# Normalisation in two batches of images, deviations by a matrix product, last output chunk in halves by images

## The reference

```python
def _gn(v, G=32, eps=1e-05):           # per image, over groups of 4 channels and all pixels
    g = v.reshape(B_, G, C_ // G, H_, W_)
    m = jnp.mean(g, axis=(2, 3, 4), keepdims=True)
    s = jnp.var(g, axis=(2, 3, 4), keepdims=True)
    return ((g - m) / jnp.sqrt(s + eps)).reshape(v.shape)

def step(h, xr):                        # 32 steps over lines, per direction
    out = _gru_step(xi, h, wih, whh)    # r, z = sigmoid(x W + h W); n = tanh(x W + r * (h W))
    ctx = out ...                       # (1 - z) * n + z * h
    h_new = jnp.tanh(_conv1d(ctx, cw, cb))   # three taps along the line
    return (h_new, ctx)

x = x + (einsum(concat([ctx_above, ctx_below, ctx_left]), w_comb) + b_comb)
```

## Time and profile before

| | |
|---|---|
| median of 3 runs | 341.11 us (340.92 to 341.3) |
| profiled execution | 341.09 us |
| its span, first to last instruction | 339.3 us |
| TensorE busy | 321.5 us (95%), 2723 products |
| VectorE busy | 291.5 us (86%) |
| ScalarE busy | 253.9 us (75%) |
| GpSimd busy | 11.0 us (3%) |
| DMA | 10.61 MB; HBM read 6.16 MB, written 4.19 MB |

### The profile page before, as it was taken

The page is one execution under the profiler, slowest core; times in us unless marked ns, Lnnn a source line. Parts: engine busy times, 40 slices in busy tenths (PEclk is TensorE's granted clock), DMA queues, the critical chain, the costliest instruction groups (busy, mean ns, idle before and its releaser), DMA issues.

```text
span 339.3 us, 7733 instructions
## 1 busy us (share of the span) xinstructions
PE 321.5 (95%) x2723; PEld 261.0 (77%) x2723; DVE 291.5 (86%) x781; ACT 253.9 (75%) x593; POOL 11.0 (3%) x24
## 2 busy tenths in 40 slices
PE   0589999999999999999999999999999999999995
PEld 0237678888888888888888888888888888874443
DVE  1889999999999999999988888889898888894542
ACT  5979899999888887887777777777777777767600
POOL 2540000000000000000000000000000000000000
PEclk9999999999999999999999999999999999999999
DMA  7900000000000000000000000000000000000655
GB/s 297 411 19 4 0 2 0 2 3 1 2 2 0 3 2 1 2 0 3 0 0 0 0 0 0 0 0 0 0 0 0 0 0 0 0 2 0 198 149 149
DMA packets 11252, 10.61 MB, mean 31 GB/s; under 512 B 2529, under 2 KB 9825, under 8 KB 11233
## 3 DMA queue, kind: packets, MB, share of 16 engines
q1 hardware_dynamic: 11232, 10.36, 9.1%
HBM read 6.16 MB, written 4.19 MB: 31 GB/s over the span
## 4 chain that ended last, share of the span: by engine, by line
PE 87%; ACT 4%; DVE 3%; DMA 2%; issue 1%; POOL 1%; POOLq 0%; SPq 0%; ACTq 0%; DVEq 0%
PE rz_bank L909 23%; PE conv_bank L909 18%; PE rz_bank L912 11%; PE n_bank L909 11%; PE conv_bank L912 9%; PE n_bank L912 6%; DMA x<-x_dram 2%; PE rz_bank L1017 1%; PE rz_bank L1021 1%; PE rz_bank L1019 1%; PE n_bank L1017 1%; PE n_bank L1021 1%; PE n_bank L1019 1%; ACT w_parts L470 1%; PE conv_bank L1021 1%
## 5 line engine op out<-in xcount | busy, mean ns | idle before, releaser
L909 PE MATMUL conv_bank<-ctx_store,w_parts 128*128 (+1 forms) x558 | 106.7, 273 | 0.4
L909 PE MATMUL rz_bank<-x_rows,w_parts 128*128 (+1 forms) x378 | 77.7, 273 | 1.0 <-DVE x_rows L662 0.5
L909 PE MATMUL rz_bank<-h_parts,w_parts 128*128 128x256 f16 x372 | 76.2, 273 | 0.3 <-DVE h_parts L771 0.3
L524 ACT ACTIVATE nval<-npre 128x256 f32<-128x256 f32 x93 | 38.6, 415 | 48.0 <-DVE npre L766 48.0
L512 ACT ACTIVATE rz<-rz_bank,descale 128x512 f32<-128x512 f32 x93 | 63.9, 687 | 8.4 <-PE rz_bank L909 1.6
L912 PE MATMUL conv_bank<-ctx_store,w_parts 128*128 (+1 forms) x279 | 66.0, 273 | 0.0
L909 PEld LDWEIGHTS conv_bank<-ctx_store,w_parts 128*128 128x128 f16 x558 | 53.8, 97 | 14.6 <-DVE ctx_store L759 1.9
L748 DVE SCALAR_TENSOR_TENSOR npre<-n_bank,descale,rz 128x256 f32<-128x256 f32 x93 | 44.9, 483 | 15.5 <-ACT rz L512 14.2
L529 ACT ACTIVATE hval<-conv_bank,biases,descale 128x256 f32<-128x256 f32 x93 | 51.4, 553 | 0.3
L912 PE MATMUL rz_bank<-x_rows,w_parts 128*128 (+1 forms) x189 | 51.5, 273 | 0.0
L909 PE MATMUL n_bank<-x_rows,w_parts 128*128 128x256 f16 (+1 forms) x192 | 47.1, 273 | 0.0
(11 more groups left out here) (99 smaller groups left out, 417.3 us busy)
## 6 DMA issues: line engine op xcount, KB each, us to landing
x<-x_dram SPq DMA_DIRECT2D x8, 512.0 KB, 8.3
out_dram<-x_rows SPq DMA_DIRECT2D x7, 512.0 KB, 3.3
ctx_store<-weights_dram SPq DMA_DIRECT2D x3, 576.0 KB, 5.1
out_dram<-x_rows SPq DMA_DIRECT2D x2, 256.0 KB, 2.6
ctx_store<-weights_dram SPq DMA_DIRECT2D x1, 192.0 KB, 12.0
biases<-biases_dram SPq DMA_DIRECT2D x1, 2.0 KB, 11.7
```

The costliest lines, as they stand in the source:

```text
L524: nc.scalar.activation(nval[k][:], npre[k][:], ACT.Tanh).then_inc(n_done[k], 1)
L909: last = nc.tensor.matmul(out, w_block(HI, k, n), parts(hi_or_lo), start=start, stop=stop and hi_or_lo == LO, skip_group_check=True)
```

## The change

**Two batches.** Mean, variance, power and shift are made for images 0 to 5 and then for 6 and 7 (`BATCHES`), each with semaphores of its own count. A new matrix `group_dev` = `unit_diag` - `group_avg`, built by GpSimd, gives the deviation from the group mean by one product; ScalarE squares it (`squared_dev`) and the variance is summed in PSUM by two products, of the channel variances and of the squares.

```diff
-            nc.tensor.matmul(avg_bank[:, 0:B], group_avg[:], meanvar[:, :, 0],
-                             start=True, stop=True).then_inc(mean_avg, 1)
-            warm(CHAIN_WARM)
-            pe.wait_ge(spread_done, 1)
-            nc.tensor.matmul(var_bank[:, 0:B], group_avg[:], dev[:], ...
+            def batch_means(batch):
+                images = slice(*BATCHES[batch])
+                by_act = sum(b < images.stop for b in ACT_IMAGES)
+                pe.wait_ge(aggr_done, images.stop - by_act)
+                pe.wait_ge(act_stats, 2 * by_act)
+                nc.tensor.matmul(dev_bank[batch][:, images], group_dev[:], meanvar[:, images, 0], ...
+                nc.tensor.matmul(mean_bank[batch][:, images], group_avg[:], meanvar[:, images, 0], ...
+                nc.tensor.matmul(var_bank[batch][:, images], group_avg[:], meanvar[:, images, 1],
+                                 start=True, stop=False)
+            def batch_variance(batch):
+                pe.wait_ge(spread_done, batch + 1)
+                nc.tensor.matmul(var_bank[batch][:, images], group_avg[:], dev[:, images],
+                                 start=False, stop=True).then_inc(var_avg, 1)
+            batch_means(0)
+            batch_variance(0)
+            batch_means(1)
+            batch_variance(1)
             turn_sums(1)
-            warm(TURN_WARM)
+            warm(5)
             spread_peaks(1)
-            warm(CHAIN_WARM)
-            pe.wait_ge(x_factor, 1)
-            warm(LAST_WARM)          # 7
+            pe.wait_ge(x_factor, 2)
+            warm(LAST_WARM)          # 4
```

```diff
 # ScalarE
-            for unit in range(2, UNITS.index("in 2")):
-                weights_hi(unit)
-            for k in (2, COMB):
-                magnitude_sums(k)
+            weights_hi(2)
+            squared_dev(0)
+            weights_hi(3)
+            weights_hi(4)
+            weights_hi(5)
+            magnitude_sums(2)
+            squared_dev(1)
+            magnitude_sums(3)
...
 # VectorE
-            for b in (2, 3, 5, 6, 7):
-                image_stats(b)
-            spread()
+            image_stats(2)
+            image_stats(3)
+            image_stats(5)
+            image_stats(6)
+            group_mean(0)
+            variance(0)
+            image_stats(7)
             weights_lo(UNITS.index("conv 1"))
-            variance()
-            sets_peak(1)
             weights_lo(UNITS.index("rec 1"))
-            shift()
...
+            shift(0)
+            normalise(2, edges)
+            group_mean(1)
+            variance(1)
+            normalise(3, edges)
+            normalise(4, edges)
+            sets_peak(1)
+            shift(1)
+            normalise(7, edges)
+            normalise(0, strip)
+            normalise(1, strip)
+            weight_scales(1)
             x_lo(FIRST_ROWS[0])
-            weight_scales(1)
+            x_lo(FIRST_ROWS[1])
+            x_lo(FIRST_ROWS[2])
             x_lo(FIRST_ROWS[3])
```

**Turn to the output.** In block (31, 2) the first four hidden products of direction 2 are issued ahead of the output products:

```diff
+                begun = j == 2 and isinstance(t, int) and t == STEPS - 1
+                if begun:
+                    hidden_gates_hi(2, STEPS - 1)
                     unit_ready("comb")
```

**Last chunk.** Both rows of images 0 to 3 and then of images 4 to 7 (`LAST_PARTS`) are multiplied into a bank each, summed, and stored singly:

```diff
-            for row in range(CHUNK_ROWS):
+            for part, (b, end) in enumerate(LAST_PARTS):
...
+            for part, (b, end) in enumerate(LAST_PARTS):
+                sp.wait_ge(y_summed, CHUNKS + part)
+                sp.dma_start(out_d[b:end, :, last * CHUNK_ROWS:CHUNKS * CHUNK_ROWS, :]
+                             .rearrange("b c h w -> c b (h w)"),
+                             y_sb[:, whole, b:end, CHUNK_ROWS * W:STORE_ROWS * W]).then_inc(y_stored, 16)
```

More of the change, by code:

```diff
@@ L382, in _ @@
                     .then_inc(y_stored, 16)
[L383 to L389, removed]
+            sp.wait_ge(y_summed, last)
+            sp.dma_start(out_d[:, :, (last - 1) * CHUNK_ROWS:last * CHUNK_ROWS, :].rearrange("b c h w -> c b (h w)"),
+                         y_sb[:, whole, :, 0:CHUNK_ROWS * W]).then_inc(y_stored, 16)
+            for part, (b, end) in enumerate(LAST_PARTS):
[3 more added lines that the diff above has]
+                             y_sb[:, whole, b:end, CHUNK_ROWS * W:STORE_ROWS * W]).then_inc(y_stored, 16)
+            sp.wait_ge(y_stored, 16 * (whole + 1 + len(LAST_PARTS)))
         @block.gpsimd
@@ L963, in input_products, with hidden_gates_hi, hidden_products @@
                     last.then_inc(n_ready[k], 1)
-            def hidden_products(k, s):
+            def hidden_gates_hi(k, s):
+                pe.wait_ge(h_hi_done[k], s)
+                for gate in range(2):
+                    passes(rz_bank[k][:, gate * COLS:(gate + 1) * COLS], k, GATES + gate,
+                           lambda part: h_parts[k][:, part, :], HI)
+            def hidden_products(k, s, begun=False):
                 def parts(part):
                     return h_parts[k][:, part, :]
-                pe.wait_ge(h_hi_done[k], s)
-                for gate in range(2):
-                    passes(rz_bank[k][:, gate * COLS:(gate + 1) * COLS], k, GATES + gate, parts, HI)
+                if not begun:
+                    hidden_gates_hi(k, s)
                 pe.wait_ge(h_lo_done[k], s)
@@ L1003, in convolution, with chunk_part @@
                 last.then_inc(conv_ready[k], 1)
-            def chunk_part(c, k, first=0, end=CHUNK_ROWS):
-                rows = slice(c * CHUNK_ROWS + first, c * CHUNK_ROWS + end)
-                out = y_bank[(c + first) % RING][:, 0:(end - first) * W * B] \
-                    .rearrange("p (h w b) -> p h w b", h=end - first, b=B)
+            def chunk_part(c, k, bank=None, b=0, end=B):
+                rows = slice(c * CHUNK_ROWS, (c + 1) * CHUNK_ROWS)
+                out = y_bank[(c if bank is None else bank) % RING][:, 0:CHUNK_ROWS * W * (end - b)] \
+                    .rearrange("p (h w b) -> p h w b", h=CHUNK_ROWS, b=end - b)
                 def ctx_part(p):
@@ L1088, in _ @@
             c = CHUNKS - 1
-            for row in range(CHUNK_ROWS):
-                pe.wait_ge(y_summed, c + row - RING + 1)
+            for part, (b, end) in enumerate(LAST_PARTS):
+                pe.wait_ge(y_summed, c + part - RING + 1)
                 for k in range(DIRS):
-                    last = chunk_part(c, k, row, row + 1)
+                    last = chunk_part(c, k, c + part, b, end)
                 last.then_inc(y_ready, 1)
```

141 lines of the change are left out of this document (82 added, 59 removed).

## The result

The changed kernel takes 342.49 us (median of 22 runs, 341.64 to 342.97), the kernel before 341.01 (22 runs). The ratio is 1.0037 with a 95% interval of 1.0031 to 1.0044: slower by 1.5 us, where 340.9 was forecast. The profiled execution took 342.26, its span 340.5 (before 339.3: +1.2). The front alone lost more than that; the two ends brought most of what was forecast of them.

The account below looks back on a forecast made before the run. The prediction took a chain of waits over VectorE, GpSimd and ScalarE to bound the kernel up to 39.6 us, then TensorE products. 341.09 + 0.6 (front) - 0.33 (turn) - 0.5 (last store) gave 340.9 us, range 339.8 to 342.9.

Parts of the forecast that it names:

- step 3: Front, VectorE's chain from the fourth weights_lo on: first x_lo at 24.9 instead of 24.23, +0.67; front +0.6 us.
- TensorE falls back: Rival: TensorE drops to 1.2 GHz in the front, five products take 2.1 instead of 1.1; 342.9 us, chance 0.16.
- Step 1: Front, TensorE reaching the first batch: deviation product at about 18.1 behind twelve slow warm-ups, variance(0) at 19.24.
- warm-up over sooner: Rival: fast spacing comes within the twelve front warm-ups, four take 0.85 less; front -0.25, 340.0 us, chance 0.16.
- step 2: Front, work queued behind new waits: image 7's statistics 2.4 us later, ScalarE idle 16.3 to 18.5, first power at 20.25.
- The power: GpSimd's power in the front: 1.24 for six columns and 0.41 for two, by column shares of 1.65; no wait added.
- the limit of 0.9: Front, GpSimd's second power, two columns: starts at 22.5, asked for at 23.4, so it may take 0.9 before it costs.
- The rival with two of 1.65: Power does not shrink with its columns: the second ends at 24.35, first x_lo at 25.8, +1.6; 341.9 us, chance 0.07.
- The turn: Loop to output products: four hidden products run in TensorE's 0.43 wait, gain 0.33 us, bounds 0 and 0.44.
- The last chunk: End of kernel: half stored after the first sum, last store only 128 KB, -0.5 us, bounds -0.6 and -0.1.
- the outer bound of +1.0: Last chunk's products: operand runs of 8 bytes taken as free, at worst a doubled read costing +1.0 us.
- The rival with the tail hidden: Gap products issued late and the half store landing as slowly as the whole: 341.7 us, chance 0.05.

Follow-up runs that it names:

- experiment 12: Changed kernel with image 7's statistics ahead of the first batch's mean and the square behind weights_hi 3 to 5, no added warm-ups: 340.24 us, in two groups.
- experiment 1: Changed kernel with nine more warm-up products, seven after batch_variance(0) and two ahead of batch_variance(1): 340.59 us, ratio to the kernel before 0.9982.
- Experiment 11: Changed kernel with image 7's statistics early, the square late, three warm-ups inside, six at the end, and first x_lo ahead of weight_scales(1): 340.30 us.
- experiment 7: Changed kernel with nine more warm-ups ahead of batch_variance(1) and image_stats(7) ahead of group_mean(0) and variance(0): 340.81 us, ratio 0.9989.
- experiment 10: Changed kernel with image 7's statistics ahead of the first batch's mean, square behind weights_hi 3 to 5, three warm-ups inside, six at the end: 339.52 us.
- experiment 4: Kernel before with only the four hidden_gates_hi products of direction 2 put ahead of the first output products: 340.61 us, ratio 0.9988.
- experiment 5: Kernel before with only the last chunk in halves by images and two stores of 128 KB: 340.60 us, ratio 0.9985.
- experiment 9: Changed kernel with 9 front warm-ups instead of 12, eight after batch_variance(0), two ahead of batch_variance(1): 341.42 us, in two groups.
- experiments 8: Changed kernel with 6 front warm-ups instead of 12, three after batch_variance(0), one ahead of batch_variance(1): 341.38 us, ratio 1.0008.
- old front with both ends: Kernel before with hidden products ahead of the output products and the last chunk in halves, nothing of the new front: 340.34 us, ratio 0.9979.
- experiment 3: Kernel before with the changed kernel's thinner warm-ups: 12 in front, none in the two places of four, 5 ahead of spread_peaks(1), 4 at the end: 341.09 us.

## Why the prediction was wrong

It moved by +1.5 where no measurable change was forecast, inside the range given.

**The step that failed** is the one that took TensorE's level as held through the front (step 3, and "they were at the fast spacing from 18.65"). Its mechanism stood among the rivals, *TensorE falls back*, with 0.16: five products at 2.1 (measured 2.31), 342.9 in all (342.49), decided by a spacing over 0.3 (0.43). The argument against it, "no stretch of more than 1.7 without a product", was no argument: the wait was 1.69 and the level fell, and in experiment 12 it fell without such a wait. What the runs support is in the rival's first sentences: where the old front had warm-up products in every microsecond, the new one has nothing but small float32 pairs from 17.2 to 22.2. The granted clock was 0.50 from 19.5 to 26.2, and experiment 1, which puts nine products into that stretch, shows the price, 1.90 of the 2.15. The Trainium skill (TensorE: Matmul & The Clock Gate, "A second HAM failure mode: psum-queue depth-cycling") has a level that goes back and forth with short idle times between groups. The trace of experiment 12 agrees in so far as the level fell with no idle time over 0.31; whether these short ones were its cause no run shows.

**Front without the clock.** The terms of steps 1 to 3 were about right where the level held: in experiment 1 the first batch comes behind twelve slow warm-ups at 18.22 (forecast 18.1), image 7's statistics at 19.62 (19.3), `x_hi` at 24.69 (24.4) and `x_lo` at 25.23 (24.9), with warm-ups that started 0.17 later than before. Step 1 let the variance product follow the square at once; two more pairs stand ahead of it in TensorE's queue, and `variance(0)` came 1.32 behind the first pair and not 1.14. In these traces the new front then costs 0.97 against the old one, 0.75 from the first warm-up on, against +0.6 forecast. By medians it is only 340.59 - 340.34 = 0.25. The rest is probably executions in which the warm-up ends earlier, as in the profiled run of the changed kernel; no such run of experiment 1 was traced. That was the rival *warm-up over sooner*; in the traced execution of the changed kernel it came true together with the fall-back, which no case had combined.

**What was queued behind the waits** (step 2) was right in kind. The prediction counted these stalls inside its +0.6 and did not ask for another order; taking both waits behind the work, with other warm-ups, brought 340.59 to 339.52 by medians and 341.29 to 340.45 in the traced executions. Experiment 11, nearly the same kernel, has 340.30.

**The power** took 1.33 for six columns and 0.80 for two, where the shares gave 1.24 and 0.41; the limit of 0.9 held and no wait came of it in the changed kernel. In experiments 7 and 10 to 12 six columns took 1.64 or 1.65, and VectorE waited 0.78 for them. The rival with two of 1.65 is out. The Trainium skill (GPSIMD Engine Reference, "Performance versus the Vector engine") has a cost for each element and, beside it, a dispatch and a join of the cores for each instruction. The rows agree that it does not go by the elements alone: 0.80 for two columns is more than half of the 1.33 for six.

**The turn**: forecast -0.33; the trace gives -0.27 to -0.32, experiment 4 -0.44. **The last chunk**: forecast -0.5; -0.46 in the trace and -0.45 in experiment 5. The reads with runs of 8 bytes cost 0.003 a product, so the outer bound of +1.0 is out. The rival with the tail hidden is refuted. Together the ends bring 0.71, a little less than their sum of 0.89, within the uncertainty of 0.3 that each ratio has.

**Open.** Which work exactly keeps the level is not settled; the runs show orders that fell and orders that did not. Nor is it shown why the first fast product comes after six or seven in one execution (the changed kernel), after twelve in another (experiment 1) and after seventeen, with four pairs among them, in a third (experiment 9), what the untraced runs of experiments 8 and 9 did, whether experiment 10 or 11 is better, and whether either is better than the old front with both ends by more than the 0.04 of experiment 11.

## What to carry to other kernels

Products whose results nobody reads can be load-bearing: before an edit thins them out or stretches the time between them, price the same stretch at both clock levels, by what waits for each product in it. When a wait is put into a queue in order, put behind it only what needs it: here image 7's statistics and three weight conversions stood behind two tiny waits, and moving them ahead took 0.3 to 1.1 us off experiment 1's time (340.30 and 339.52 against 340.59). An edit whose times fall in two groups has not been measured by its median; read the granted clock of each group (it tells them apart in experiment 12 and not in experiment 9), and trace a run of each.

## What was unexpected of the hardware

- The level fell to 0.50 with TensorE never idle for over 0.31 us in the 7 us before (experiment 12), its work there being warm-ups until 17.8, then pairs of 0.36, and the first two of the five warm-ups from 20.43.
- The price of a fall differs between executions of one kernel: in experiment 12 about 0.7 us in the traced one (0.995), and 2.2 between the groups. In the thinned kernel of experiment 3 six executions with a mean clock of 0.993 to 0.995 were as fast as those with 1.00.
- The mean granted clock can be 0.999 or 1.000 in runs 2 us apart (experiment 9), and it reads 1.00 over products 0.43 apart.
- The power of GpSimd took 1.65 for eight columns, 1.33 for six in the changed kernel and experiment 1, 1.65 for six in experiment 7, straight behind its other work in all three, 1.64 for six after 1.53 idle (experiment 10), and 0.80 for two: neither a price a column nor a fixed one, and the two durations for six are not explained, and spans of GpSimd are rough.
- A store of 128 KB took 2.2 to 2.3 from issue to landing, one of 256 KB 2.6 to 2.7: half the bytes save 0.4, and at 215 GB/s the flow of 128 KB is 0.6.
